# Earlier first steps, a new order of VectorE and ScalarE work in attention, and a new place for the first FFN weight splits

## The reference, cut to what is computed

```python
x = x + cross_attention_0(layernorm(x), ctx)   # RMS norm and rotary on q and k, 16 heads, 4 key groups, causal
x = x + ffn_0(layernorm(x))                    # 1376 hidden columns, a rank-8 side path, 8 expert side paths of rank 8, top 2
x = x + similarity(layernorm(x), ctx)          # kv = ctx @ Wk; softmax(layernorm((p @ kv) @ kv.T))
x = x + moe(layernorm(x))                      # 64 experts, top 8, 192 hidden columns, at most 128 rows each
```

## Time and profile before

| what | us |
|---|---|
| median of the three runs | 1283.7 |
| the profiled execution | 1284.93 |
| its span | 1283.1 |
| TensorE matmuls busy | 1193.3 (93%) |
| VectorE busy | 723.9 (56%) |
| ScalarE busy | 527.3 (41%) |
| GpSimd busy | 483.4 (38%) |
| mean granted TensorE clock | 0.984 of full |

### The profile page before, as it was taken

How to read it: one execution, slowest core, us unless ns; L and a number is a source line. 1 busy time by engine, 2 the same in 40 slices (tenths; PEclk the granted TensorE clock), 3 DMA queues, 4 the chain that set the end, 5 groups by cost and what they waited for, 6 DMA issues and landing times.

```text
span 1283.1 us, 19538 instructions
## 1 busy us (share of the span) xinstructions
PE 1193.3 (93%) x6575; PEld 863.3 (67%) x6575; DVE 723.9 (56%) x1476; ACT 527.3 (41%) x1194; POOL 483.4 (38%) x541
## 2 busy tenths in 40 slices
PE   4899999999999999999999999999899999999990
PEld 3667777667777766777776687777456666666650
DVE  6966565686687678677868857554722222222220
ACT  4875221776412278542237853222333333333320
POOL 0440233462123446113353602121255555555530
PEclk8999999999999999999999999999999999999995
DMA  8012231002333000313300013632789999999847
GB/s 294 4 61 78 108 108 63 1 1 102 110 125 116 34 1 2 142 68 139 105 32 1 35 69 113 229 148 109 288 270 332 360 360 349 347 358 357 216 57 140
DMA packets 45906, 187.04 MB, mean 146 GB/s; under 512 B 6716, under 2 KB 9788, under 8 KB 31364
## 3 DMA queue, kind: packets, MB, share of 16 engines
q1 hardware_dynamic: 30964, 146.18, 30.2%
q0 software_dynamic: 14864, 39.85, 13.5%
HBM read 155.31 MB, written 34.90 MB: 148 GB/s over the span
## 4 chain that ended last, share of the span: by engine, by line
PE 73%; DVE 13%; ACT 5%; DMA 3%; issue 2%; POOL 2%; DVEq 0%; SPq 0%; POOLq 0%; ACTq 0%
PE PS L2568 14%; PE PS L1986 10%; PE PS L1988 10%; PE PS L1987 10%; PE PS L2584 4%; PE PS L2074 3%; PE PS L2588 3%; ACT P L892 3%; PE PS L2093 3%; DVE NM L1424 3%; PE PS L2558 2%; PE PS L2005 2%; DMA WRAW<-in_ffn 2%; PE PS L2385 1%; PE PS L2384 1%
## 5 line engine op out<-in xcount | busy, mean ns | idle before, releaser
L2568 PE MATMUL PS<-WE,XGT 128*128 128x384 f32 x512 | 192.7, 499 | 1.5 <-issue 1.5
L712 POOL CAST HH<-HID 128x512 fp32r<-128x512 f32 x44 | 37.3, 847 | 330.8 <-DVE HID L1792 330.8
L1019 ACT ACTIVATE WHI<-WRAW 128x1280 fp32r<-128x1280 f32 x44 | 56.0, 1273 | 226.5 <-DMA WRAW<-in_ffn 226.5
L1986 PE MATMUL PS<-XTH,WHI 128*128 128x512 f32 x352 | 141.1, 401 | 3.4 <-DVE WLO L1735 3.4
L1988 PE MATMUL PS<-XTH,WLO 128*128 128x512 f32 x352 | 138.2, 393 | 0.0
L1987 PE MATMUL PS<-XTL,WHI 128*128 128x512 f32 x352 | 137.9, 392 | 0.0
L892 ACT ACTIVATE P<-PS,NM 128x512 f32<-128x512 f32 (+3 forms) x256 | 131.9, 534 | 13.9 <-DVE NM L1424 12.9
L2568 PEld LDWEIGHTS PS<-WE,XGT 128*128 128x128 f32 x512 | 87.1, 190 | 56.7 <-issue 22.5
L1970 DVE COPY HMT<-PS 128x256 f32<-128x256 f32 x64 | 27.2, 425 | 163.8 <-PE PS L2577 159.3
L1424 DVE TENSOR_REDUCE NM<-PS 128x2 f32<-128x1024 f32 (+2 forms) x96 | 98.6, 1041 | 31.4 <-PE PS L1995 31.2
L2074 PE MATMUL PS<-ident,P 128*128 128x128 f32 x640 | 93.9, 278 | 14.8 <-ACT P L892 7.0
(11 more groups left out here) (341 smaller groups left out, 2733.1 us busy)
## 6 DMA issues: line engine op xcount, KB each, us to landing
WE<-in_we SPq DMA_DIRECT2D x64, 1152.0 KB
WRAW<-in_ffn SPq DMA_DIRECT2D x44, 1060.0 KB, 5.0
acc<-HN SPq DMA_DIRECT2D x17, 256.0 KB, 5.1
XIN<-in_x SPq DMA_DIRECT2D x4, 1024.0 KB, 6.4
out<-X SPq DMA_DIRECT2D x4, 1024.0 KB, 5.1
out<-acc POOLq DMA_DIRECT2D x1, 4096.0 KB, 23.0
hx<-HN SPq DMA_DIRECT2D x3, 1152.0 KB, 4.5
CTX<-in_ctx SPq DMA_DIRECT2D x4, 256.0 KB, 2.9
```

Source lines behind the costliest of these rows:

```text
L1019: act.activation(WHI[slot][:, 0:WD], WRAW[slot][:, 0:WD], ACT.Copy).then_inc(S["wg_hi"], 1)
L1986: pe.matmul(dst, a[0], b_[0], start=first, stop=False, **kw)
L2568: mm = pe.matmul(bank(2 + s % 2, 0, 2 * F1), XGT[s % 2][:, k, :], WE[s][:, k * 2 * F1:(k + 1) * 2 * F1], start=(k == 0), stop=(k == KC - 1))
```

## The change

- **Loads.** `x` of the first batch comes as two transfers (tiles 0 and 1, then 2 and 3), each with a semaphore. The tables keep one semaphore and come as key norm, key cosine and sine, query cosine and sine, query norm.
- **First steps.** VectorE aggregates the context's statistics before it looks at `x`; GpSimd takes the powers in that order. The shift of `x`'s rows is worked out inside `first_keys`, which no longer waits for it.
- **Semaphores.** The first increments of 23 semaphores are given by ScalarE and of 27 by TensorE, in place of GpSimd.
- **Unneeded matmuls.** 38 (of zeros) right at the start, ahead of the wait for the tables, and 6 between the first two turned stacks, in place of 10 after the tables.
- **Attention.** In `g = 2` ScalarE copies the first block of t = 2 out, not VectorE. In pass 0 and in `g = 2` of the others VectorE copies stack 2 and ScalarE stack 3 (before: the other way round), stack 2 right after the t = 2 blocks. In `g = 1` of the others VectorE copies the key stack before the last maximum. In `g = 3` two statistics (`stats_x3` of tiles 1 and 2) go behind the copy of the first t = 1 blocks. `exp_y(2)` goes behind stack 3.
- **Projection of pass 0.** Two tiles, not three, have their first three k parts ahead of the last group.
- **FFN entry.** VectorE does `wg_rest(0)` before all low parts of the turned rows. ScalarE does `wd_hi(0)` and `wg_hi(1)` between the norms of rows 0, 1 and the copies of the turned rows. VectorE does `wd_rest(0)` and the parts of `wg_rest(1)` between the later low parts, its end after the expert weights. ScalarE does `wg_hi(2)` before `wd_hi(1)`, and VectorE `wg_rest(2)` before `HID` of chunk 1 and `wd_rest(1)` after it.
- **Clears.** The five clearing matmuls go; the first product of each bank starts it.

```diff
@@ sync
-                sp.dma_start(XIN[:, :, :], rows(x_rows, NT)).then_inc(S["x_loaded"], 16)
+                if b == 0:
+                    sp.dma_start(XIN[:, 0:2, :], rows(x_rows, NT)[:, 0:2, :]).then_inc(S["x_first"], 16)
+                    sp.dma_start(XIN[:, 2:NT, :], rows(x_rows, NT)[:, 2:NT, :]).then_inc(S["x_loaded"], 16)
...
@@ gpsimd
-                if name not in BY_DMA:
+                if name not in BY_DMA | BY_ACT | BY_PE:
                     pool.sem_inc(S[name], 1)
-                part = slice(NT, 2 * NT) if n == 1 else slice(0, NT)
+                part = slice(0, NT) if n == 1 else slice(NT, 2 * NT)
@@ turning_order
-            order += [("P", g, 2, 0, 1, "a" if g == G - 1 else "d"), ("P", g, 2, 1, 1, "a")]
+            order += [("P", g, 2, 0, 1, "a" if g > 1 else "d"), ("P", g, 2, 1, 1, "a")]
-                order += [("stack", g + 1, 2, "a"), ("stack", g + 1, 3, "d")]
+                order += [("stack", g + 1, 2, "a" if tail and g < 2 else "d"), ("stack", g + 1, 3, "d" if tail and g < 2 else "a")]
@@ scalar, ffn
+                    if half == 0:
+                        act.wait_ge(S["dn_ps"], 1 + b * NF)
+                        wd_hi(0)
+                        wg_hi(1, 1, b * N1 + 1)
+                    else:
...
-                    if not (isinstance(f, int) and f < 2):
-                        act.wait_ge(S["dn_ps"], 1 + b * NF + f - 1)
-                    wd_hi(slot)
-                    silu(f)
                     if f == 1:
                         act.wait_ge(S["up_ps"], 1 + b * NF + 1)
                         wg_hi(2, 0, next_loads)
-                wg_hi(1, 1, b * N1 + 1)
+                    if f > 1:
+                        act.wait_ge(S["dn_ps"], 1 + b * NF + f - 1)
+                    if f > 0:
+                        wd_hi(slot)
+                    silu(f)
@@ vector, front_norms
                 dve.wait_ge(S["ctx_loaded"], 16 * (fb + 1))
+                aggregates(0, statistics(0, NT))
...
+                if fb == 0:
+                    dve.wait_ge(S["x_first"], 16)
+                    statistics(NT, NT + 2)
+                dve.wait_ge(S["x_loaded"], 16 * (fb + 1))
+                aggregates(NT, statistics(NT + 2 if fb == 0 else NT, 2 * NT))
@@ vector, first_keys
                 fstep.post(turned(ka, 0, HD, ck, 0, HD))
+                between()
                 fstep.post(turned(kb, ROT, HD, sk, 0, ROT))
@@ vector, attention
-                        n = stats_x3(b, 1)
-                    if g < G - 1:
+                    if g < 2:
                         turned(g, 2, 0)
                     if sims:
                         similarity_scales(b)
                         y(0)
+                        stack(g + 1, 0, KST)
                     maximum(g, 5)
...
                     turned(g, 1, 0, 2)
+                    if norm:
+                        stats_x3(b, 1)
+                        n = stats_x3(b, 2)
@@ vector, ffn
+                wg_rest(0, 0)
                 turned_rest(0)
                 shifts(b, 2, 2, 4)
                 turned_rest(1)
-                wg_rest(0, 0)
+                dve.wait_ge(S["dn_ps"], 1 + b * NF)
+                wd_rest(0, 0)
+                wg_begin(1, 1)
                 turned_rest(2)
+                wg_part(1, 0, WB1 // 2)
                 turned_rest(3)
...
+                wg_low = wg_part(1, WB1 // 2, WB1)
...
-                    if not last and f > 1:
+                    if not last and f > 0:
                         wg_rest(f + 1, 1 - slot)
-                    wd_rest(f, slot)
+                    if f > 1:
+                        wd_rest(f, slot)
...
                     if f == 1:
-                        wg_rest(2, 0)
-                wg_rest(1, 1)
+                        wd_rest(1, 1)
+                step.need(wg_low)
+                wg_end(1, 1)
@@ tensor
                 stack(0)
+                if fb == 0:
+                    keep_clock(7, FILL[1])
                 stack(1)
...
-                for t in range(NT - 1):
+                for t in range(NT - 1 if tail else 2):
                     if t == 1:
                         inverse(G - 1)
                     projected_out(t, 2 if tail and t == 1 else 0, KC - 1)
...
-                    projected_out(t, KC - 1, KC).then_inc(S["op_ps"], 1)
+                    projected_out(t, KC - 1 if tail or t < 2 else 0, KC).then_inc(S["op_ps"], 1)
...
-                clear(6, 7, 2)
                 down_first()
...
+            pe.wait_ge(setup_dve, 1)
+            unread(7, FILL[0])
             pe.wait_ge(tables_loaded, TABLES_LOADED)
-            keep_clock(7, 10)
```

More of the change, by code:

```diff
@@ L287, in build @@
     ZR = HN[:, 0, :]
+    ZB = ZR.bitcast(BF16)
     WE = []
@@ L848, in _ @@
         def _(act):
+            for name in sorted(BY_ACT):
+                act.sem_inc(S[name], 1)
             def query_rows(t, c0, c1):
@@ L1528, in attention @@
                     turned(g, 2, 3)
+                    if g < G - 1 and not (rows_in or sims):
+                        stack(g + 1, 2, QST[1])
                     if rows_in:
@@ L2395, in gate_up @@
                     lora(f, slot, 1)
-                def clear(*banks):
-                    for bk in banks:
-                        pe.matmul(bank(bk), zrow[:, 0:P], zrow[:, :], start=True, stop=False, skip_group_check=True)
                 def down_first():
@@ L2411, in ranks_down @@
                         for part in w:
-                            pe.matmul(bank(2, parts=LR), part[:, WAD:WAD + LR], h[:, :], start=False, stop=False,
-                                      skip_group_check=True)
+                            pe.matmul(bank(2, parts=LR), part[:, WAD:WAD + LR], h[:, :],
+                                      start=(h is HH[0] and part is hi), stop=False, skip_group_check=True)
                     pe.wait_ge(S["wd_lo"], 1 + b * NF + 1)
@@ L2540, in last_tail, with unread @@
                 last_list()
+            def unread(bk, n):
+                for _ in range(n):
+                    pe.matmul(bank(bk), ZB[:, 0:P], ZB[:, P:P + 512], start=True, stop=True)
+            pe.wait_ge(setup_dve, 1)
+            unread(7, FILL[0])
             pe.wait_ge(tables_loaded, TABLES_LOADED)
-            keep_clock(7, 10)
             first_group(0)
```

115 lines of the change are left out of this document (60 added, 55 removed).

## The result

Over four runs each, the changed kernel took 1271.24 us (median, 1270.35 to 1271.93), the kernel before 1284.03 us on the same chip: a ratio of 0.9903, with a 95% interval from 0.9888 to 0.9917. It is 12.8 us faster, where 4.95 us were forecast. The range held the time by 0.2 us, at the end that the first rival had set; the forecast itself missed more than half of the gain. The profiled execution has a span of 1270.1 us, 13.0 us less than before.

What follows compares the result with a forecast made beforehand. TensorE, busy 93% of the span, was taken as the bound, so only its ended waits count: start -2.9, attention 0 -0.3, attentions 1 to 3 -2.4, FFN passes +0.65, sum -4.95 us, median 1278.7 us; range 1271.0 to 1281.9.

Steps and rivals of the forecast that it cites:

- the first rival: FFN chunk 1: VectorE gets its turn before GpSimd, each pass gains 1.6 us, 1272.9 us in all; chance 0.25.
- Start: Up to the first row maximum: keys start at about 11.3 us, first query at 14.15; gains 2.9 us, bounds 1.5 and 3.6.
- The late landing of the halves, the pessimistic bound: Kernel start: by the transfer-size rule the last byte of `x` comes later in two halves, 1.4 us less gain.
- Attention 0: First attention: only `g = 2`, with no query work, gains; 0.3 us, bounds 0 and 2.
- attentions 1 to 3: Later attentions: 0.2 us in `g = 1`, 0 in `g = 2`, 0.6 in `g = 3`; 2.4 us in all.
- Entry of pass 0: FFN entry, pass 0: two ScalarE parts come before the turned rows are copied, projections start later; 1.25 us lost.
- Chunks 0 and 1: FFN, each pass: `HID` of chunk 1 waits behind `wg_rest(2)`, slowed by GpSimd; 0.15 us a pass left of 2.5.
- the three gains of 2.5 us a pass: FFN chunks 0 and 1: chunk 1's weight stop, the clears and the stop before chunk 2 go; 2.5 us a pass.
- GpSimd is no obstacle: FFN chunk 1: VectorE gets its turn first, FFNs gain 6.4 - 1.25 = 5.15 us, 1272.9 us in all; chance 0.25.
- The sign named ahead: Each pass: a TensorE stop of 1 to 2.5 us before the second half of `down_first`, ended by `HID`.
- The slower rival, chunk 3's weights: FFN: second buffer's refill late, TensorE stops in each of four passes; 2.1 us each gives 1287.1 us; chance 0.04.
- the start gives little: Kernel start: late tables or `x` halves, or a clock fallback, give 1.0 us, not 2.9; 1280.6 us; chance 0.17.

## Why the prediction was right or wrong, point by point

- **Start, -2.9 against -3.66 us: the size was off by a quarter.** The mechanism held: the keys start with the last table (11.01 us, forecast 11.3), the first query follows at 13.81 us (forecast 14.15), the first maximum at 21.76 us (forecast 22.1). That the matmuls of zeros would have raised the clock by then holds too (1.00 from 14 to 22 us), but is worth 0.3 to 0.7 us. The 50 increments matter, as it said: undoing them costs 1.0 us, though more than half of that through TensorE, whose filling then ends too early. The halves of `x` are worth 0.6 us in the one execution that was tried without them, in which `x` landed early. The late landing of the halves, the pessimistic bound, never came up.
- **Attention 0, -0.3 against -0.38, and attentions 1 to 3, -2.4 against -3.1.** The term of 0.6 us in `g = 3` was measured at 0.60 by undoing it, and TensorE's stop there fell from 1.16 to 0.56 us. `g = 1` gave 0.14 for a forecast 0.2. `g = 2`, put at nothing, gave 0.3 in each of three attentions: that is the missed part, and no run took it apart.
- **Entry of pass 0, +1.25 against +1.30; passes 1 to 3, 0 against 0 (within 0.1).** Right in place, cause and size: the two parts of ScalarE's stand ahead of the turned rows.
- **Chunks 0 and 1, -0.15 against -1.6 to -2.2 us a pass: this step failed.** It read: "subtraction held to 345.6 and done at 346.8, GpSimd's scaling until 348.0, the last addition (0.5 us) until 348.5, `HID` until 349.2". Everything before it in the argument was right: the three gains of 2.5 us a pass, that `HID` would be the new wait, and that GpSimd's reads would lengthen it. What was wrong is who issues first. VectorE's subtraction comes directly behind its cast, and GpSimd's low part 10 ns later; so VectorE is held once and not twice. When a wait of 0.1 us turned the order round, the forecast's course appeared to within half a microsecond (a stop of 2.00 us for 2.45), with 4.5 us more of stops in four passes.
- **The rivals.** "GpSimd is no obstacle" named this outcome, 1.6 us a pass, at a chance of 0.25; with it the sum is 1272.9 us, and the larger gains of the start and of `g = 2` are most of what is left to 1271.24. Its `HID` end of 347.75 came out as 347.8, once the 5.78 us by which this trace was ahead at chunk 0 are added. The argument against it was that GpSimd had won at 348.65 "in just that position". But there its subtraction had begun 0.18 us ahead, and in the new order the two issue times followed from steps that I rounded to 0.1 us and more. So one order was no better founded than the other, and the chance should have been near a half. The sign named ahead, a stop of 1 to 2.5 us, spans both orders, since the rival's own numbers give 347.75 - 346.75 = 1.0 us; it could not tell them apart. The slower rival, chunk 3's weights, didn't occur: but the chain has less slack than the 2.6 us worked out at chunk 3, since a delay of 1.74 us stopped TensorE at chunk 5, behind VectorE's work on the expert lists, which the forecast's working left out. The rival "the start gives little" was out.
